# Decoder kernel, context attentions: probabilities turned as two query halves on two row strips, two units at a time

## The reference

```python
# L0 cross: 16 heads of 8.  L1 cross: 8 heads of 64, four layers of it.  L3 cross: 16 heads of 64.
q, k, v = split_heads(x @ Wq), split_heads(ctx @ Wk), split_heads(ctx @ Wv)
sim  = einsum('bhid,bhjd->bhij', q, k)      # [512, 154] per head, scaled, masked in L3
a    = softmax(sim, axis=-1)
out  = einsum('bhij,bhjd->bhid', a, v)      # needs a with the keys on the partitions
out  = merge_heads(out) @ Wo
```

## Time and profile before

| | |
|---|---|
| median of 3 runs | 4510.98 us (4506.9 to 4514.82) |
| profiled execution, its own time | 4516.42 us |
| its span, first to last instruction | 4514.8 us |
| PE busy | 4015.5 us (89%) |
| DVE busy | 2675.4 us (59%) |
| ACT busy | 1998.7 us (44%) |
| mean granted TensorE clock | 0.955 of full speed |

### The profile page before, as it was taken

How to read it: one execution, slowest core, us unless ns; L and a number is a source line. 1 busy time by engine, 2 the same in 40 slices (tenths; PEclk the granted TensorE clock), 3 DMA queues, 4 the chain that set the end, 5 groups by cost and what they waited for, 6 DMA issues and landing times. The chain is left out here.

```text
span 4514.8 us, 70500 instructions
## 1 busy us (share of the span) xinstructions
PE 4015.5 (89%) x23856; PEld 2483.2 (55%) x23856; DVE 2675.4 (59%) x7163; ACT 1998.7 (44%) x5804; POOL 860.4 (19%) x972
## 2 busy tenths in 40 slices
PE   6887799999999988889968877999999999888898
PEld 4644445655555555555646444565555555555555
DVE  3677566666666644654346775666666666456543
ACT  1732435555445434663227214454554444346632
POOL 2145221122221200000021452211122212000000
PEclk7999999999999998999969999999999999999999
DMA  2000000000000010010010000000000000100000
GB/s 68 24 16 1 16 7 16 22 16 22 16 22 1 25 54 19 7 57 8 1 57 5 16 1 16 7 16 22 16 22 16 22 2 24 54 20 34 30 8 10
DMA packets 15847, 91.84 MB, mean 20 GB/s; under 512 B 2176, under 2 KB 8064, under 8 KB 12032
## 3 DMA queue, kind: packets, MB, share of 16 engines
q1 hardware_dynamic: 15488, 87.27, 5.3%
HBM read 86.22 MB, written 1.05 MB: 19 GB/s over the span
## 5 line engine op out<-in xcount | busy, mean ns | idle before, releaser
L559 PE MATMUL ps_O<-wide,V 128*64 128x256 f32 (+4 forms) x5152 | 596.5, 394 | 1.9 <-ACT wide L583 1.8
L628 ACT ACTIVATE EX<-NB,neg 128x154 f32<-128x154 f32 (+3 forms) x640 | 350.2, 551 | 399.4 <-DVE neg L653 399.2
L601 POOL COPY RX<-recips 128x256 f32<-128x256 f32 (+2 forms) x356 | 156.8, 440 | 1822.9 <-DVE recips L668 1757.2
L679 DVE TENSOR_TENSOR QT<-ps_O,RS 128x512 f32<-128x512 f32 x212 | 146.6, 692 | 444.3 <-PE ps_O L559 444.3
L510 PE MATMUL ps_S<-KT,QT 64*128 64x154 f32 (+7 forms) x1936 | 368.0, 463 | 31.8 <-issue 21.5
L583 ACT ACTIVATE wide<-ps_P 128x512 f32<-128x512 f32 (+2 forms) x648 | 367.6, 569 | 60.9 <-PE ps_P L541 60.8
L394 POOL TENSOR_TENSOR small<-small 128x4 f32<-128x4 f32 x112 | 113.5, 1013 | 1467.8 <-DVE small L379 955.1
L541 PE MATMUL ps_P<-consts,EX 128*128 128x128 f32 (+1 forms) x2148 | 317.3, 281 | 80.0 <-ACT wide L583 41.5
L559 PEld LDWEIGHTS ps_O<-wide,V 128*64 128x64 f32 (+4 forms) x5152 | 266.9, 127 | 194.5 <-issue 110.7
L510 PE MATMUL ps_OUT<-KT,QT 64*128 64x154 f32 (+5 forms) x968 | 336.0, 441 | 0.4 <-ACT EX L628 0.4
L585 DVE COPY wide<-ps_P 128x512 f32<-128x512 f32 (+4 forms) x404 | 259.3, 643 | 117.9 <-PE ps_P L541 117.5
(11 more groups left out here) (345 smaller groups left out, 8154.1 us busy)
## 6 DMA issues: line engine op xcount, KB each, us to landing
weights<-in_w_dram SPq DMA_DIRECT2D x10, 1664.0 KB, 6.8
weights<-in_w_dram SPq DMA_DIRECT2D x2, 6148.0 KB, 17.5
weights<-in_w5next_dram SPq DMA_DIRECT2D x6, 1664.0 KB, 6.8
weights<-in_w_dram SPq DMA_DIRECT2D x2, 4200.0 KB, 13.0
weights<-in_reltab_dram SPq DMA_DIRECT2D x2, 4096.0 KB, 12.3
weights<-in_w_dram SPq DMA_DIRECT2D x8, 640.0 KB, 3.9
weights<-in_w_dram SPq DMA_DIRECT2D x5, 832.0 KB, 4.4
weights<-in_w_dram SPq DMA_DIRECT2D x2, 2050.0 KB, 8.0
```

Source lines behind the costliest of these rows:

```text
L559: ins = pe.matmul(O1[self.slot * j:self.slot * (j + 1), q0 * P:(q0 + self.nq) * P], self.value(c * self.hpc + j, kc), self.probs(rd, j)[:, ...
L601: pool.tensor_copy(RX[:, q0 * P:(q0 + self.nq) * P].rearrange("p (n s) -> p n s", s=self.slot), of.unsqueeze(2).broadcast_to([P, self.nq * ...
L628: ins = act.activation(ex[:, a * N:(a + 1) * N], src, ACT.Exp, bias=neg[:, at:at + 1], scale=-1.0 if self.added else 1.0, accum_out=sums[: ...
L679: dve.tensor_tensor(self.out_chunk(c), O1[:, :], RS[:, c % 2, :], ALU.mult).then_inc(r.av_sb, 1)
```

## The change

In the three context attentions two units (0 and 1, then 2 and 3) are turned together. Each transpose [128, 77] to [77, 128] becomes two of [64, 77] to [77, 64]: queries 0 to 63 on the row strip 0 to 63, queries 64 to 127 on the strip 64 to 127, the identity's 64 x 64 diagonal blocks streaming. The lower halves of both units go to the first of two banks and the upper halves to the second, so that a pair fills the same two banks as before, in another arrangement. A pair begins when both units' exponentials are done and when the two items before the last one in the ring (positions s-3 and s-2) are copied out. The copy out of unit k takes one half of the queries of both units. The wait for a free `exes` buffer is for the whole pair.

```diff
+                self.halved = self.ctx
...
-                        for k in range(4):
+                        if self.halved:
+                            for k in (0, 2):
+                                self.turn_pair(pe, r, rd, k)
+                        for k in range(0 if self.halved else 4):
...
+            def turn_pair(self, pe, r, rd, k):
+                pe.wait_ge(r.exped, 4 * rd + k + 2)
+                nb = len(self.banks)
+                s = self.first[rd] + k
+                for half in range(2):
+                    if s + half >= nb:
+                        self.evacuated(pe, r, s + half - nb)
+                N = self.width(self.item(rd, k)[0])
+                blocks = [(u, kc, a) for u in range(2) for kc in range(N // self.kc) for a in range(self.w)]
+                for b, (u, kc, a) in enumerate(blocks):
+                    ex = self.exes[(4 * rd + k + u) % len(self.exes)]
+                    for half in range(2):
+                        rows_ = slice(64 * half, 64 * half + 64)
+                        ins = pe.transpose(self.banks[(s + half) % nb][0:self.kc, b * 64:(b + 1) * 64],
+                                           ex[rows_, a * N + kc * self.kc:a * N + (kc + 1) * self.kc],
+                                           ident[rows_, rows_])
+                        if b == len(blocks) - 1:
+                            ins.then_inc(r.probsT, 1)
+
+            def turned_of(self, n):
+                return n // 2 * 2 + 2 if self.halved else n + 1
...
-                dst = self.probs(rd, j)[:, 0:n, at:at + w]
-                src = self.banks[s % len(self.banks)][0:self.kc, 0:n * w].rearrange("p (c q) -> p c q", c=n)
+                bank = self.banks[s % len(self.banks)]
+                if self.halved:
+                    qts, j = self.item(rd, k // 2 * 2)
+                    at, m, half = (qts[0] % self.nq) * P, self.nch * self.nq * P, k % 2
+                    of = 2048 * (rd % 2) + j * m
+                    dst = wide[0:self.kc, of:of + 2 * m].rearrange("p (u c q) -> p u c q", u=2, c=self.nch)
+                    dst = dst[:, :, :, at:at + w].rearrange("p u c (a q) -> p u c a q", a=self.w)
+                    dst = dst[:, :, :, :, 64 * half:64 * half + 64]
+                    src = bank[0:self.kc, 0:n * w].rearrange("p (u c a q) -> p u c a q", u=2, c=n, a=self.w)
+                else:
+                    dst = self.probs(rd, j)[:, 0:n, at:at + w]
+                    src = bank[0:self.kc, 0:n * w].rearrange("p (c q) -> p c q", c=n)
...
-                                act.wait_ge(r.probsT, n - len(self.exes) + 1)
+                                act.wait_ge(r.probsT, self.turned_of(n - len(self.exes)))
```

## The result

| | before | after |
|---|---|---|
| median, 4 runs each on one chip | 4512.15 us (4506.9 to 4514.82) | 4707.85 us (4706.11 to 4709.41) |
| profiled execution, span | 4514.8 us | 4705.3 us |
| mean granted TensorE clock | 0.955 | 0.911 |

After over before is 1.0435 [1.0417, 1.0453]: 196 us slower, where 23 were forecast and 4600 was the top of the range. Beside the first experiments one run of before took 4720.09 us at a mean clock of 0.910; it is left out of the ratios, and the six others there took 4507 to 4516.

The account below looks back on a forecast made before the run. Each round was taken as bound by a loop over PE and ACT, its last wait being for turn0. Terms 10.8 + 3.8 + 3.9 + 1.4 + 3.5 = 23.4 us gave 4534 us (+0.5%), range 4510 to 4600.

Parts of the forecast that it names:

- Step 1: PE's work: blocks of 0.067 us make a pair 0.536 instead of 0.872, saving 86 us of PE time.
- Step 2: All three attentions: second pair waits for turn0, with 0.536 us after it instead of 0.436; +0.10 a round, 10.8 us.
- Step 3: First pair ready 0.09 later, mode change 0.10: L3Cross 3.8 us, L1Cross with L3Cross's last round 3.9, L1Cross round 0 1.4.
- Step 4: L3Cross's round 1: first pair waits for the last round's turn3; next exponential +0.87 us, 4 executions, 3.5 us.
- The copies: Copies out of the transposes: same elements in runs of 64 instead of 256, turn0 stays 0.58 us, no cost.
- PE's saved time: Rival: PE's own order sets the round, so the 86 us saved arrive: 4425 us, with half 4468; 11%.
- The block bound by the stream (0.054): Rival: a block takes 0.054 us, a pair 0.43; sum +5 us, 4516, the same by measurement; 15%.
- the load that does not shrink (0.111): Rival: a block takes 0.111 us, a pair 0.89; +86 us, 4597; 12% together with strips in turn.
- the strips that take turns (0.134): Rival: strips don't overlap, a block takes 0.134 us; about +120 us, 4631; 12% together with the unshrinking load.

Follow-up runs that it names:

- isolated runs: The change made in one attention alone, medians against before: L3Cross 4630.94 us (1.0258), L1Cross 4536.15 us (1.0033), L0Cross 4569.65 us (1.0122).
- filler kernel: The changed kernel plus full identity transposes between the pairs, 6 a round in L0Cross, 3 in L1Cross, 12 in L3Cross: 4569.28 us, 1.0134 of before.
- fewer: Kernel before with the pair's waits and full transposes, only each unit's first query tile turned (4 of 8 per pair): 4580.6 us, 1.0141 of before.
- one-strip version: The changed kernel with all blocks of a pair's lower strip first, then all of the upper: 4773.53 us, 1.0555 of before.
- the order alone: Kernel before with the change's waits and its full transposes kept: 4576.05 us, 1.0142 of before.

## Why the prediction was wrong

- *The missing step.* "The 2 x 0.336 = 0.67 us saved per round turn into idle time before the second pair" was the right reading of the path, and its price was put at nothing. That was the failed step: no term of the sum let PE's own speed depend on what it does. The array's work in a round became less, and the clock was at 1.2 GHz for 158 us of L0Cross and 220 us of L3Cross. In the isolated runs these two stages cost 57 and 120 of the 196 us; between first and last values they cost 50.6 and 107.9, where the filler kernel, with the same waits and blocks and the clock held (but for those 12 us of L0Cross), has 4.4 and 12.7 over before. The profile of before held the warning: the clock line starts at 7, PE came to L0Cross at 1.2 GHz and rose to 2.4 only 3.5 us before the first values, and the mean of 0.955 showed a clock that moves with the work. I had noted the 0.955 and not asked what a lighter round would do to it.
- *Step 1, a block.* 0.067 forecast, 0.069 measured, both strips at once. An estimate from the Trainium skill, "TensorE: Matmul & The Clock Gate", LDWEIGHTS, was 0.064; the trace agrees roughly. What I missed is a pair's first block, 0.12 to the second: it makes a pair's first to last start 0.53 instead of 0.47.
- *Step 2, the wait.* Right in place: 0.14 to 0.15 us behind turn0. The size was +0.12 in L1Cross and +0.14 in L3Cross instead of +0.10. In L0Cross it was 0: the filler's steady rounds there take 5.16 and 4.68 us from values to values, before 5.16 and 4.67. In before the second group of the scores' weight loads waits 0.24 us for ACT's exponentials; in the filler kernel it does not wait, and this gives back what the pair takes.
- *Step 3, readiness.* The change of mode was 0.10 as forecast (0.59 for 0.49). The exponential behind the pair started 0.19 later than behind T0, not 0.09; the pair's last block ends 0.76 after its first start, where I had 0.69. An L3Cross round costs +0.43 instead of +0.29. L1Cross's rounds, from values to values, cost +0.21, +0.34 and 0, where I had 0.10 to 0.22.
- *Step 4.* Right. L3Cross's second turning round in the filler kernel, ACT's turn3 and then PE's first pair, 0.15 behind its end (before, T0 ran ahead of turn3). The next exponential starts 1.00 behind turn3's end, where the step made 0.92 and before has 0.22:

```profile
1956.43 0.57 ACT L638 ACTIVATE wide<-ps_P 77x512 f32<-77x512 f32 x1
```

```profile
1957.15 0.25 PE L601 MATMUL ps_O<-consts,EX 64*77 64x64 f32 x1 [0.77 <-ACT wide L638]
```

- *The copies.* As forecast, 0.58 to 0.59 for turn0.
- *The rivals.* None had the cause. PE's saved time did not arrive, for the reason given: T3 stood behind turn0 and not only near it. The block bound by the stream (0.054), the load that does not shrink (0.111) and the strips that take turns (0.134) are refuted by the 0.069.
- *What stays open.* The filler version, whose clock holds in L3Cross and nearly in L0Cross, is 58 us over before, where the steps make 23. Of the 53 us between the two profiled spans that I can place, 12.7 lie in L3Cross, 15.3 in and between the L1 stages, 4.4 in L0Cross, and 21 ahead of and behind the stages, where low clock grew by some 60 us; that last part was not taken apart. What exactly of the array's work counts towards the clock is open too: rows times columns streamed are alike in "fewer" and in after, and after fell further. In L3Cross missing work and longer idle time were not separated. Filler in the form of strips was not tried.

## What to carry to other kernels

Before PE work is taken out of a loop whose end another engine sets, look at the granted clock of that stretch and at what PE has left in it: here 86 us less of PE work became 196 us more time, most of it by a lower clock for everything else in the loop. A cheap test for it is useless work in the gap: if the kernel gets faster and the granted clock rises, it was the clock. A gap in front of a wait is better filled with work that stands behind it in the order; here this made the kernel before 0.8% faster with all transposes kept.

## What the hardware showed that was not expected

- The granted clock was at 1.2 GHz for most of a stretch beside short idle times and a busy PE. In after's L3Cross PE was busy 63.20 of 74.70 us at a mean clock of 0.65, with waits of 2.15 us; in its L0Cross 41.98 of 46.60 at 0.52, where the longest idle time is 0.77 us, six times in the execution; in the one-strip version 48.84 of 50.00 at 0.52. The first of these six on PE:

```profile
225.41 0.36 PE L585 MATMUL ps_O<-consts,EX 64*77 64x64 f32 x1 [0.77 <-ACT wide L622]
```

- Array instructions are not equal in this. With 0.87 us of full transposes in a pair (the order alone) L0Cross was low for 0 of 132 us, with 0.94 us of blocks mostly one strip at a time for 197 of 202.
- Full transposes alone did bring the clock back: 0.52 to 1.00 in L0Cross's second execution with 6 a round, 0.65 to 1.00 in L3Cross with 12. The Trainium skill, "TensorE: Matmul & The Clock Gate", Part 4 (PE-mode transpose), says that transposes don't count as PE-busy in the same way. Those in float32 of these runs counted, and the measurement decides.
